# Three layers of a graph network: the low parts of gathered rows made in four pieces instead of one, and matmuls that wait piece by piece

## The reference

```python
def _mean_aggregate(x, src, dst, n_nodes):
    msg = x[src]
    summed = jax.ops.segment_sum(msg, dst, num_segments=n_nodes)
    deg = jax.ops.segment_sum(jnp.ones((src.shape[0],), x.dtype), dst, num_segments=n_nodes)
    return summed / jnp.maximum(deg, 1.0)[:, None]

def _sage_conv(x, src, dst, Wl, bl, Wr, n_nodes):
    mean_nb = _mean_aggregate(x, src, dst, n_nodes)
    return mean_nb @ Wl.T + bl + x @ Wr.T
...
x = _layernorm(x + _L0_gnn_ref(x, edge_index, edge_type_500, ...), axis=-1)
h = relu(_sage_conv(x, src, dst, W1l, b1l, W1r, n))
h = relu(_sage_conv(h, src, dst, W2l, b2l, W2r, n))
x = _layernorm(x + _sage_conv(h, src, dst, W2l, b2l, W2r, n), axis=-1)
```

## Time and profile before

| | |
|---|---|
| device time, median of 3 (range) | 3848.27 us (3825.55 to 3861.35) |
| span of the profiled execution (first to last instruction) | 3293.7 us |
| PE busy in the span | 2864.3 us (87%) |
| DVE busy | 2458.8 us (75%) |
| POOL busy | 2351.4 us (71%) |
| ACT busy | 2224.0 us (68%) |
| gathers of layers 1 to 3 (line 1483, table_h), 1,128 | 1236.6 us |
| row lows (line 1824), 282 | 343.1 us |
| row matmuls (line 2012), 2,256 | 344.9 us |
| dense matmuls (line 2052), 4,116 | 945.7 us |
| mean granted clock of PE | 0.935 |

### The profile page before, as it was taken

The page is one execution under the profiler, slowest core; times in us unless marked ns, Lnnn a source line. Parts: engine busy times, 40 slices in busy tenths (PEclk is TensorE's granted clock), DMA queues, the critical chain, the costliest instruction groups (busy, mean ns, idle before and its releaser), DMA issues. The chain is left out here.

```text
span 3293.7 us, 54777 instructions
## 1 busy us (share of the span) xinstructions
PE 2864.3 (87%) x16731; PEld 2464.3 (75%) x16731; DVE 2458.8 (75%) x5529; ACT 2224.0 (68%) x3945; POOL 2351.4 (71%) x2185
## 2 busy tenths in 40 slices
PE   6559999999999989997599999669999957999985
PEld 4448877787778878786488888558888846888884
DVE  7968888888888888887466667546666745787786
ACT  1057777777777777774577877468877836777771
POOL 6267777777777777773577777567777756777773
PEclk6579999999999999998799999889999978999997
DMA  4256666665556666663766666376666647666662
GB/s 136 73 133 168 173 165 167 167 167 165 167 164 168 165 173 167 168 169 113 228 196 201 199 194 188 105 246 207 201 195 197 184 134 225 204 210 205 206 185 89
DMA packets 335600, 573.59 MB, mean 174 GB/s; under 512 B 47029, under 2 KB 231686, under 8 KB 335302
## 3 DMA queue, kind: packets, MB, share of 16 engines
q0 software_dynamic: 101088, 277.97, 30.4%
q1 hardware_dynamic: 230697, 289.55, 28.1%
q10 hardware_dynamic: 3517, 2.48, 0.3%
HBM read 491.85 MB, written 77.97 MB: 173 GB/s over the span
## 5 line engine op out<-in xcount | busy, mean ns | idle before, releaser
L1483 POOL DMA_INDIRECT rows_arena<-table_h,src_idx x1128 | 1236.6, 1096 | 483.8 <-issue 364.0
L2052 PE MATMUL bank<-wide_counts,h_pairs 128*128 128x512 f32 (+1 forms) x4116 | 945.7, 384 | 123.6 <-ACT wide_counts L1632 104.0
L1483 POOL DMA_INDIRECT rows_arena<-table_scaled_x,src_idx x782 | 839.0, 1073 | 285.8 <-issue 273.6
L2052 PEld LDWEIGHTS bank<-wide_counts,h_pairs 128*128 128x128 f32 x4116 | 735.4, 193 | 262.9 <-issue 128.3
L1989 PE MATMUL bank<-rel_pairs,ftype_hot 125*128 125x258 f32 x4688 | 711.0, 299 | 51.3 <-ACT ftype_hot L1610 51.0
L1989 PEld LDWEIGHTS bank<-rel_pairs,ftype_hot 125*128 125x128 f32 x4688 | 620.6, 191 | 85.5 <-ACT ftype_hot L1610 51.1
L1632 ACT CAST wide_counts<-rows_arena 128x1024 fp32r<-128x1024 bf16 (+1 forms) x525 | 549.8, 1047 | 68.0 <-DMA rows_arena<-edge_counts 67.9
L1832 DVE TENSOR_TENSOR h_pairs<-rows_arena,h_pairs 128x512 fp32r<-128x512 f32 (+1 forms) x525 | 352.9, 682 | 259.6 <-ACT h_pairs L1629 254.9
L1824 DVE TENSOR_TENSOR row_pairs<-rows_arena,row_pairs 128x1024 fp32r<-128x1024 f32 x282 | 343.1, 1218 | 208.8 <-ACT row_pairs L1619 202.5
L1629 ACT CAST h_pairs<-rows_arena 128x512 fp32r<-128x512 f32 (+1 forms) x525 | 320.9, 611 | 197.3 <-PE bank L2052 152.9
L1653 ACT CAST rows_arena<-bank 128x448 bf16<-128x448 f32 (+1 forms) x812 | 368.3, 505 | 119.3 <-PE bank L2038 74.9
(11 more groups left out here) (186 smaller groups left out, 3098.9 us busy)
## 6 DMA issues: line engine op xcount, KB each, us to landing
rows_arena<-edge_counts SPq DMA_DIRECT2D x234, 512.0 KB, 4.0
edge_counts<-fcount SPq DMA_DIRECT2D x52, 832.0 KB, 6.3
rows_arena<-in_edge_type_dram SPq DMA_DIRECT2D x195, 187.5 KB
rows_arena<-table_h SPq DMA_DIRECT2D x36, 512.0 KB, 11.9
rows_arena<-table_h,src_idx POOLq DMA_INDIRECT x1128, 3.6
rows_arena<-table_scaled_x,src_idx POOLq DMA_INDIRECT x782
table_h<-chunk_info SPq DMA_DIRECT2D x96, 128.0 KB, 4.0
rows_arena<-edge_counts SPq DMA_DIRECT2D x39, 256.0 KB, 3.1
```

Of the source, the lines that this page charges most:

```text
L1483: pool.indirect_dma_start(out=rows[:, g % ring, c, :], out_offset=None, in_=table[:, :], in_offset=bass.IndirectOffsetOnAxis(ap=src_idx[:, ...
L2052: last = pe.matmul(bank[2 + h][:, 0:cols_of(w)], h_pairs[:, v % HALVES, part, b % HALF, h * P:(h + 1) * P], wide_counts[:, v % HALVES, b % ...
```

## The change

In layers 1 to 3, `row_lows` makes the same low parts with four DVE instructions of 128x256, one per chunk, in place of one of 128x1024; the first waits for `s_row_hi` as before, and each raises `s_row_lo` by one, so the semaphore now counts chunks. `sums` on PE no longer has one wait ahead of a quad's 8 matmuls, but one ahead of each chunk's 2. POOL's wait before it reuses a slot is rewritten to the new count: it still waits for all four pieces of quad g - 4. Layer 0, ACT, and every other instruction are as before.

```diff
--- before.py
+++ after.py
@@ -1477,7 +1477,10 @@
                     def _(pool):
                         for g in range(groups):
                             if g >= ring:
-                                pool.wait_ge(s_free if first else s_row_lo, g - ring + 1)
+                                if first:
+                                    pool.wait_ge(s_free, g - ring + 1)
+                                else:
+                                    pool.wait_ge(s_row_lo, GC * (g - ring + 1))
                             for c in range(chunks_of(g)):
                                 col = g * GC + c
                                 pool.indirect_dma_start(
@@ -1821,9 +1824,10 @@
                         def row_lows(g):
 
                             dve.wait_ge(s_row_hi, g + 1)
-                            dve.tensor_tensor(row_pairs[:, g % ROW_PAIRS, 1, :, :], rows[:, g % ring, :, :],
-                                              row_pairs[:, g % ROW_PAIRS, 0, :, :].bitcast(F32),
-                                              ALU.subtract).then_inc(s_row_lo, 1)
+                            for c in range(GC):
+                                dve.tensor_tensor(row_pairs[:, g % ROW_PAIRS, 1, c, :], rows[:, g % ring, c, :],
+                                                  row_pairs[:, g % ROW_PAIRS, 0, c, :].bitcast(F32),
+                                                  ALU.subtract).then_inc(s_row_lo, 1)
 
                         def half_lows(v):
 
@@ -2006,8 +2010,8 @@
                                                      msg[:, g % MSGS, c, 0:sum_cols], start=(g % GW == 0 and c == 0),
                                                      stop=(g == last_quad(w) and c == n - 1))
                             else:
-                                pe.wait_ge(s_row_lo, g + 1)
                                 for c in range(n):
+                                    pe.wait_ge(s_row_lo, GC * g + c + 1)
                                     for part in range(2):
                                         last = pe.matmul(seg_bank[w % 2][:, 0:sum_cols], hot[:, g % HOTS, c, :],
                                                          row_pairs[:, g % ROW_PAIRS, part, c, :],
```

## The result

The changed kernel took 3911.09 us (median of 4 runs, 3901.30 to 3923.49) where the kernel before, timed beside it, took 3840.49 us (median of 4, 3825.55 to 3861.35). The ratio is 1.0187, with a 95% interval of 1.0148 to 1.0226. Forecast were 3821 us and a range of 3796 to 3855. So the change costs 1.9% here, the forecast had it 0.7% faster, and the result lies outside the range.

What follows compares the result with a forecast made beforehand. PE was taken to bound each layer's steady part, POOL its last dozen quads. Layer ends -28, last quads -2, `add_dense` +3 gave -27 us: span 3267 plus 554.6 made 3821 us, against 3848.3; range 3796 to 3855.

Steps and rivals of the forecast that it cites:

- with 554.6 us around it, the distance from span to median: Whole kernel: 554.6 us taken to lie outside the profiled span and added to the new span of 3267 us.
- Both are near their limit, and they take turns.: Layers 1 to 3: PE bounds while dense units last, POOL's gather issue bounds the last dozen quads.
- so this lies in its idle time: DVE's row lows: the 65 us more DVE time from four pieces is hidden, as DVE waits for ACT ahead of most.
- The rival "slower": DVE and POOL: the lock passes from piece to piece, 52 us more on POOL, 3900 us; chance 7%.
- PE's waits at nothing: PE's row matmuls: three more waits per quad, 846 in all, cost nothing; 20 ns each would be 17 us.
- The loss to low parts: POOL's gathers: time lost to holds by low parts, 114 us in all before and 31 us with pieces.
- POOL's 84 us: POOL's gathers: shorter holds gain POOL 0.30 us per quad, 84 us in all, a pitch of 1.33 us instead of 1.41.
- So at quad 82 it will have issued 348: POOL in each layer: its lead when PE starts quad 82 grows to 5 quads, 348 gathers, from 344 or 341.
- POOL's gain is swallowed: Rival on POOL: its lead at quad 82 can't grow, so no change, 3840 us; chance 14%.
- the 28 us that the larger lead was to give behind quad 82: Layer ends: fewer gathers left, each shorter, gain 8 us each in layers 1 and 2 and 12 in layer 3.
- layer 3's 12 us: End of layer 3: the gathers left after quad 82 take 37 us instead of 49, a gain of 12 us.
- `add_dense`, for which the sum had 3 us more: PE's waits for `add_dense` between passes: later low parts aren't hidden there and cost 3 us, at most 4.

Runs made afterwards that it cites:

- e1: The kernel before, run again unchanged with a profile of its own, in a long set: 3772.34 us, ratio 1.0008.
- e12: Kernel before with one BN_STATS of 128 columns, read by nothing, ahead of each whole low part, in a short set: 3299.03 us, ratio 1.0009.
- e14: Kernel before with one BN_STATS of 128 columns, read by nothing, ahead of each whole low part, in a long set: 3793.57 us, ratio 1.0057.
- e16: Kernel before with three one-column memsets, read by nothing, ahead of each whole low part, in a long set: ratio 1.0054.
- e9: The changed kernel once more, against the kernel before in a short set: 3276.11 us, ratio 0.9936.
- e3: Kernel before with PE's waits by chunk; the whole low part raises the semaphore by four; long set: 3776.81 us, ratio 1.0045.
- e10: Changed kernel with PE's single wait per quad, four pieces each signalling, against the kernel before in a short set: 3281.02 us, ratio 0.9956.
- e5: Kernel before with the low part in two pieces of 512 columns, only the second signalling, in a short set: 3272.73 us, ratio 0.9919.
- e11: Two pieces of 512 columns, only the second signalling, against the kernel before in another short set: 3272.31 us, ratio 0.9929.
- e8: Kernel before with two 128x128 TENSOR_SCALARs, read by nothing, ahead of each whole low part, in a short set: 3571.40 us, ratio 1.0786.
- e6: Kernel before with three one-column memsets, read by nothing, ahead of each whole low part, in a short set: 3295.88 us, ratio 0.9985.
- e17: Kernel before with three one-column TENSOR_TENSORs of two SBUF inputs ahead of each whole low part, in a long set: ratio 1.0111.

## Why the prediction was wrong

**The step that failed** is the one before the sum: "with 554.6 us around it, the distance from span to median". Next to nothing lies around a span: it is 3907.6 of 3910.18 us in the changed kernel, 3774.5 of 3777.11 in e1. Those 555 us were inside the timed executions, as idle time and half clock of PE in every layer (layer 0 takes 1685 us in e1 and 1398 in the profile of before). So the sum was made for an execution of the short kind, and the time was taken in the long. The warning stood in the text itself, a median 17% above the one profile. Shown is that the premise failed, and that the sign of the change turns with the kind of execution (0.9936 and 1.0187). Why pieces cost in the long kind is shown in part only. With the premise fell two readings that were right for the profile alone:

- *"Both are near their limit, and they take turns."* In e1 POOL waits 264 us for low parts in place of 48, and 442 in the changed kernel, so the 36 us by which gathers got shorter (1128 x (1079 - 1047) ns) went into waiting.
- *"so this lies in its idle time"*, of DVE's 65 us. The time of one BN_STATS was free in the short kind (e12, 1.0009) and stood at 0.6% in the long (e14), where three instructions without time cost nearly as much (e16), a price that the prediction had at nothing. The rival "slower" was there at 7%, but for another mechanism and another price: it had the lock passed on in every quad, for 52 us on POOL, and it was passed on in 12 to 20 of 1,128 gathers in the six traces with four pieces, for 20 to 31 us. In the long kind POOL waited for slots far longer than that (442 us in the changed kernel).

**What held**, step by step: pieces at 0.43 us with a pitch of 0.34 (416 ns and 0.335); a gather held by one piece only, in all but some 2% of those that were held (14 of 643 in e9); PE's waits at nothing (e3's interval holds 1, and e9 is no slower than e10). The loss to low parts was put at 114 us before and 31 after, and was 123 and 57. The Trainium skill's advice for tiles of 512 or more (VectorE: DVE Perf Modes, the errata) is what two pieces follow, and their ratios are under those of four in either kind (0.9919 and 0.9929 against 0.9936; 1.0127 against 1.0187 to 1.0276, the latter in other sets; the nearest intervals overlap); what a further piece adds was measured at 0.07 us (e5's and e9's rows), as each overlaps the next by 0.08 us.

**The size, where the model's premise held.** In the short kind the sum said -27 and e9 gave -20, but mostly by the wrong places, so that the size came near is in good part luck. *POOL's 84 us* were 46, (1096 - 1055) ns x 1128: the 57 us that gathers lost in pieces are 24 of passed-on holds and 33 of the kind that the prediction counted (it had 31), and 22 us more than before were lost in one-hot matrices and half lows, into which the freed gathers ran. *"So at quad 82 it will have issued 348"*: it had issued 344, 344 and 340, and 344 in each layer of e5, e10 and e11, so the lead stayed at 4 quads, as the rival "POOL's gain is swallowed" had it, and POOL waited 101 us for low parts in place of 48. Of the 28 us that the larger lead was to give behind quad 82, 4.9 came; layer 3's 12 us didn't (its last part took 55.6 in place of 54.6 us), and there 18 of the 24 us of passed-on holds lie. Instead 17.8 us came in the steady stretches, which the prediction held to be bound by PE and gave nothing: of PE's idle time there 3.4 us less were waits for low parts, 3.5 less were waits for `add_dense`, for which the sum had 3 us more, and with the idle time went some half clock. PE's waits for low parts behind quad 82 were to go down to 8 us a layer; they are 9.1, 8.7 and 16.3.

## What to carry to other kernels

Hold the profiled execution's own time against the median first; if they are far apart, the profile is of another kind of execution, and which engine bounds the kernel has to be asked anew in the timed kind before any edit is priced. An edit that trades one engine's hidden time for another's speed is only as good as the slack in that trade, here 0.6% faster in short sets and 2% slower in long ones. Where two-input VectorE instructions hold GpSimd's gathers, two pieces of 512 got the whole gain of four of 256 in this kernel.

## What the runs showed of the hardware

- The same program took 3298 and 3296 us in two sets on one chip, and 3766 to 3847 on three others, with equal busy times of DVE and ACT in the steady stretches. In e1 67 of 129 casts on ACT begin over 0.2 us behind PE's recorded release, after idle time of up to 10 us; in the profile of before each of 100 begins 38 ns or less behind it.
- A gather held by a two-input DVE instruction mostly gets in between it and the next and ends 0.82 us behind its end. In some the hold is passed on: 1 of 524 held gathers in the profile of before, 14 of 643 in e9 (one through six instructions, 3.72 us), 196 of 404 in e8. Two TENSOR_SCALARs per quad so cost 7.9%, one of them 0.5%.
- One-column memsets on DVE start 8 ns apart and don't put off the low part behind them (e6, e16), a one-column TENSOR_TENSOR of two SBUF inputs puts off the next instruction by 0.07 us (e17). Three such memsets per quad stood at 0.9985 in a short set and at 1.0054 in a long one.
